# A transformer block with a routed feed-forward layer: three pieces of TensorE's order put elsewhere

## What is computed

```python
q = x @ wq_lat @ wq_heads            # k and v alike; 16 heads of 8
att = softmax(where(causal, q @ k.T * SCALE, -inf))
x = x + layernorm((att @ v) @ w_proj + b_proj)
ys = geglu(xn @ Ws1 + bs1) @ Ws2 + bs2           # shared part; geglu(a, g) = a * gelu(g)
top_val, top_idx = top_k((xn @ Wr + br) / 1.5, 2)
yr = sum over the two experts of softmax(top_val) * (geglu(xn @ We1[e] + be1[e]) @ We2[e] + be2[e])
x = x + layernorm(ys + yr)
```

## Time and profile before

| | us |
|---|---|
| median of 3 runs | 1270.77 |
| lowest and highest | 1266.59, 1272.27 |
| the profiled execution | 1269.61 |
| its span, first to last instruction | 1267.8 |

### The profile page before, as it was taken

The page is one execution under the profiler, slowest core; times in us unless marked ns, Lnnn a source line. Parts: engine busy times, 40 slices in busy tenths (PEclk is TensorE's granted clock), DMA queues, the critical chain, the costliest instruction groups (busy, mean ns, idle before and its releaser), DMA issues.

```text
span 1267.8 us, 31490 instructions
## 1 busy us (share of the span) xinstructions
PE 1074.8 (85%) x8446; PEld 619.5 (49%) x8446; DVE 837.0 (66%) x2411; ACT 745.3 (59%) x1311; POOL 631.4 (50%) x1184
## 2 busy tenths in 40 slices
PE   4789999999999999978888877655899999999765
PEld 2633333333333333323565545322788888888732
DVE  7587777777878777766875556322466666666637
ACT  3777777777767777756544344321566666666616
POOL 4256666666666666644145545554144444444344
PEclk9799999999999999989767887778899999999988
DMA  8223333333333333332611111111222222221156
GB/s 221 69 74 88 96 101 101 91 90 97 95 94 93 96 101 99 91 104 62 223 31 39 37 37 35 37 37 56 51 67 61 62 66 60 62 67 51 47 192 215
DMA packets 135607, 107.47 MB, mean 85 GB/s; under 512 B 32204, under 2 KB 127875, under 8 KB 135539
## 3 DMA queue, kind: packets, MB, share of 16 engines
q1 hardware_dynamic: 124722, 87.45, 24.6%
q0 software_dynamic: 8544, 17.78, 3.9%
q10 hardware_dynamic: 2272, 1.45, 0.4%
HBM read 55.96 MB, written 50.69 MB: 84 GB/s over the span
## 4 chain that ended last, share of the span: by engine, by line
PE 62%; DVE 10%; issue 9%; another core or an unknown queue 7%; ACT 7%; DMA 3%; SPq 1%; ACTq 1%; POOL 0%; DVEq 0%; POOLq 0%
PE ps L1221 11%; PE ps L1386 7%; PE ps L1387 7%; PE ps L1398 7%; DVE maxima L1524 5%; PE ps L1149 5%; PE ps L1180 5%; PE ps L1140 2%; PE ps L1313 2%; PE ps L1332 2%; PE ps L1157 2%; ACT quad_area L973 2%; PE ps L1203 1%; ACT outT_area L918 1%
## 5 line engine op out<-in xcount | busy, mean ns | idle before, releaser
L1524 DVE TENSOR_REDUCE maxima<-ps 128x8 f32<-128x1024 f32 x320 | 387.0, 1222 | 122.6 <-PE ps L1149 109.3
L911 ACT ACTIVATE pT_area<-ps 128x1024 f32<-128x1024 f32 x320 | 327.5, 1025 | 145.1 <-PE ps L1180 144.5
L699 POOL TENSOR_SCALAR_AFFINE_SELECT pT_area<-pT_area 128x256 f32<-128x256 f32 (+1 forms) x448 | 190.4, 439 | 110.9 <-ACT pT_area L911 109.1
L801 POOL DMA_INDIRECT ys_dram<-quad_area,place_cur x139 | 133.1, 957 | 206.3 <-issue 138.2
L791 POOL DMA_INDIRECT xs_dram<-quad_area,idx_cur x128 | 123.3, 963 | 139.5 <-issue 73.0
L1221 PE MATMUL ps<-pT_area,quad_area 128*32 128x512 f32 (+3 forms) x2048 | 190.9, 446 | 0.0
L1180 PE MATMUL ps<-quad_area 64*128 64x512 bf16 (+3 forms) x1024 | 124.9, 301 | 25.5 <-DVE maxima L1524 22.2
L1386 PE MATMUL ps<-quad_area 128*128 128x256 f32 (+1 forms) x456 | 129.8, 367 | 8.1 <-issue 6.8
L1387 PE MATMUL ps<-quad_area 128*128 128x256 f32 (+1 forms) x456 | 128.4, 363 | 0.0
L1149 PE MATMUL ps<-quad_area 61*128 61x128 bf16 (+2 forms) x1792 | 126.8, 244 | 0.0
L1819 DVE SCALAR_TENSOR_TENSOR quad_area<-ps,be_cur,xnT 128x256 f32<-128x256 f32 (+1 forms) x228 | 97.5, 458 | 40.2 <-ACT xnT L1009 37.1
(11 more groups left out here) (237 smaller groups left out, 1665.0 us busy)
## 6 DMA issues: line engine op xcount, KB each, us to landing
qk_dram<-split_area SPq DMA_DIRECT2D x192, 128.0 KB, 2.3
quad_area<-qk_dram SPq DMA_DIRECT2D x256, 96.0 KB, 2.3
row_area<-xs_dram SPq DMA_DIRECT2D x63, 132.0 KB
pT_area<-ys_dram SPq DMA_DIRECT2D x16, 512.0 KB, 5.2
pT_area<-in_L_ffn_We SPq DMA_DIRECT2D x12, 384.0 KB, 7.5
out_dram<-pT_area SPq DMA_DIRECT2D x7, 512.0 KB, 2.9
xs_dram<-row_area SPq DMA_DIRECT2D x5, 528.0 KB, 4.2
split_area<-in_L_ffn_We SPq DMA_DIRECT2D x12, 192.0 KB, 3.8
```

The source lines that it names most:

```text
L699: return pool.affine_select(out=blocks, in_=blocks, compare_op=ALU.is_ge, fill=0.0, base=0, pattern=[[0, count], [1, P]], channel_multipli ...
L801: pool.indirect_dma_start(ys_dram, at, ys[:, ns % 2, h, :], None).then_inc(s_yst[ns % 2], 16)
L911: act.activation(pT[:, gs % 2, n, :], ps[:, bank:bank + 2, :].rearrange("p a b -> p (a b)"), ACT.Exp).then_inc(s_exp, 1)
L1524: dve.tensor_reduce(to, ps[:, bank:bank + 2, :].rearrange("p a (j k) -> p a j k", k=P), AX, ALU.max).then_inc(s_mxf, 1)
```

## The change

Three pieces of PE's order move.

1. The third value product (kb 2) of a quad stood behind exp 4, a step after the quad's own; now it stands behind max 0 of the step after that, so behind `project` too where there is one.
2. The turn of the maxima stood behind exp 1; from step 0 on it now stands behind max 2, the next item.
3. The shared layer's second product is done a step later (batch n-9 in step n), and stands ahead of the turn of rows. ACT's copy of it (L958) follows. The stage gets one more step, which holds the last product alone; the padding copies stay in the step where they were.

```diff
-PRODUCTS = {("exp", 0): (2, 3), ("exp", 2): (1, 0), ("exp", 3): (1, 1), ("exp", 4): (1, 2)}
+PRODUCTS = {("max", 0): (2, 2), ("exp", 0): (2, 3), ("exp", 2): (1, 0), ("exp", 3): (1, 1)}
...
-        STEPS = B + 8
+        STEPS = B + 9
...
-                if ns == STEPS - 1:
+                if ns == B + 7:
                     pad(act, range(1, E, 2))
...
-                if 0 <= ns - 8 < B:
-                    act.wait_ge(s_y2, n - 7)
-                    act.activation(tiles4(ysum, n - 8), ps[:, Y2, :].rearrange("p (t c) -> p t c", c=C), ACT.Copy).then_inc(s_ysum, 1)
+                if 0 <= ns - 9 < B:
+                    act.wait_ge(s_y2, n - 8)
+                    act.activation(tiles4(ysum, n - 9), ps[:, Y2, :].rearrange("p (t c) -> p t c", c=C), ACT.Copy).then_inc(s_ysum, 1)
...
-                    if (kind, n) == ("exp", 1) and present("max_rows", gs):
+                    if (kind, n) == (("exp", 1) if gs < 0 else ("max", 2)) and present("max_rows", gs):
                         turn_maxima(gs, g)
...
                 if 0 <= ns < B:
                     turn_y(ns, n)
+                if 0 <= ns - 9 < B:
+
+                    par = (ns - 9) % 2
+                    pe.wait_ge(s_hid, 2 * n - 16)
+                    ge(pe, s_ysum, n - 9)
+                    bias(Y2, 1)
...
                 if 0 <= ns - 3 < B:
                     if ns == 3:
                         pe.wait_ge(s_yq, QUADS)
...
-                if 0 <= ns - 8 < B:
-
-                    par = ns % 2
-                    pe.wait_ge(s_hid, 2 * n - 14)
-                    ge(pe, s_ysum, n - 8)
-                    bias(Y2, 1)
```

More of the change, by code:

```diff
@@ L1295, in shared @@
                     turn_y(ns, n)
+                if 0 <= ns - 9 < B:
[3 more added lines that the diff above has]
+                    bias(Y2, 1)
+                    for t in range(NT):
+                        for j in range(2):
+                            last = pe.matmul(ps[:, Y2, t * C:(t + 1) * C], hid[:, par, j, t * P:(t + 1) * P], ws2[:, j, :],
+                                             start=False, stop=(t == NT - 1 and j == 1))
+                    last.then_inc(s_y2, 1)
                 if 0 <= ns - 3 < B:
@@ L1304, in shared @@
                     last.then_inc(s_xT2, 1)
-                if 0 <= ns - 8 < B:
-                    par = ns % 2
-                    pe.wait_ge(s_hid, 2 * n - 14)
-                    ge(pe, s_ysum, n - 8)
-                    bias(Y2, 1)
-                    for t in range(NT):
-                        for j in range(2):
-                            last = pe.matmul(ps[:, Y2, t * C:(t + 1) * C], hid[:, par, j, t * P:(t + 1) * P], ws2[:, j, :],
-                                             start=False, stop=(t == NT - 1 and j == 1))
-                    last.then_inc(s_y2, 1)
                 if 0 <= ns - 3 < B:
```

## The result

The changed kernel takes 1292.53 us (median of 4 executions, 1291.65 to 1303.58) where the kernel before, run beside it, takes 1268.68. The difference of the medians is 24 us. The ratio is 1.0211, with a 95% interval of 1.0156 to 1.0266, so the loss lies between some 20 and 34 us. The forecast was 1278.0 with a range of 1258 to 1288: the right sign, less than half of the size, and the measured time is above the range.

A forecast was written before the change was run, and what follows sets the result against it. It took PE and, after the projection, DVE's maxima to bound attention, and a 14.91 us loop through POOL's scatters the shared stage. Sum: 1269.61 + 8.4 (value product) + 0 + 0 = 1278.0 us, range 1258 to 1288.

The forecast's parts named there:

- Third value product: Attention: moving it behind max 0 costs +0.60 us per four-step loop (0.35 to 0.70), 14 times, +8.4 us.
- Turn of the maxima: Attention: the wait ahead of max 2 goes, but exp 2 still waits for DVE's second maximum; 0 us.
- Second product: Shared stage: scatters hold the second gelu's signal, so steps stay 14.91 us; 0 us, ends -5 and +8.
- first rival: "Merged scatters", shared stage: short steps alternate with long holds, +1.2 for each of four pairs, +3 at end; 1286, chance 0.17.
- The second rival: Shared stage: PE's backlog, not scatters, is the hold, so moving the second product shortens steps; 1250, chance 0.17.
- One more step: End of shared stage: the last second product and its copy, 0.60 us on ACT, hidden by 2.8 us; 0.

The follow-up runs named there:

- g4: Kernel before with the third value product behind max 0 only in steps that follow no projection: 1258.52 us (one execution).
- e1: Kernel before with only the third value product moved behind max 0: 1283.64 us, ratio 1.0069.
- e2: Kernel before with only the turn of the maxima moved behind max 2: 1255.15 us, ratio 0.9866.
- e3: Kernel before with only the shared layer's second product moved a step later, with the added step: 1272.89 us, ratio 1.0058.
- p1: Kernel before without the shared layer's second product except its bias row (shared output missing from the result): 1258.81 us (one execution).
- p2: Kernel before with four idle masks on POOL between the fourth and fifth scatter of each batch: 1241.67 us (one execution).
- g1: Kernel before with the turn of the maxima behind max 2 and four idle POOL masks between fourth and fifth scatter: 1237.50 us, ratio 0.9799.
- g3: As g1, with three idle masks in place of four: 1230.70 us, ratio 0.9750.
- e4: Changed kernel with the third value product back behind exp 4, the other parts kept: 1269.42 us, ratio 0.9986.
- f2: As e2, with POOL waiting ahead of each batch's scatters until PE's a product of this step is done: 1256.03 us, ratio 0.9911.
- h3: Changed kernel, all three parts, with three idle POOL masks in the middle of each batch's scatters: 1254.84 us, ratio 0.9910.
- h1: As g3, with two idle masks in place of three: 1243.65 us, ratio 0.9831.
- h2: As g3, with the three idle masks ahead of a batch's first scatter in place of ahead of the fifth: 1232.57 us (one execution).

## Why the prediction fell short

**Third value product: right in place and mechanism, 3 us too small.** It said +0.60 per loop. The wait ahead of max 0 was forecast at 0.99 and is 0.96; the waits on L1157 for DVE were forecast at 12.6 and are 12.4; exp 2 comes 3.98 us behind max 0, 0.67 later than before. The joins of like steps are 34.47 apart where 34.3 was forecast. The term that was mis-sized is the loss per loop: 0.80, of which 0.67 is the step after the second projection, 0.10 is the step after it, without a projection, which I had put at nothing (g4), and 0.04 lies in the step with `gs` mod 4 of 1. Fourteen times 0.80 is 11.2, and the first L973 is 11.5 later. That these agree so closely is in part luck: e1, with the same loop, has 14.9. The upper bound of 0.70 was too low since only one step had been worked through.

**Turn of the maxima: right in attention.** 0 us, with ACT's wait turned into DVE's; e1 and the changed kernel have the same loop, e2 and before too. That alone it would make the whole kernel 13 us faster, by way of the shared stage's last bursts, no term of the sum had.

**Second product: the step that failed.** The working said that the second gelu's signal is held until the scatters end, so that the second product, which isn't in the loop, changes nothing: 0 us with +8 as its end. The hold was right and its rule was wrong. A signal is not held for the whole burst: those of PE's first matmuls in it come within 2 us (the second g product of the changed kernel is over by 689.43, its gelu starts at 691.29), and those of later ones wait. In the eight equal steps of the kernel before the second gelu's g product was on the late side, and that is why 14.91 stood eight times. The change let the second product run ahead, the first gelu came 4.9 us earlier, the second one's signal slipped through at 7.2 us into the burst, and the next eight scatters joined on. This was the first rival ("merged scatters"), whose condition and shape came true: short steps that alternate with long holds. It had been given 0.17, on the ground that the eight equal steps showed no signal getting through; but those steps were of the order before, and the prediction itself had noted that the first gelu would come 2 to 3.5 us earlier. Its price was near in all and wrong in its parts: it had four pairs at +1.2 and +3 at the end, 7.8. The trace has two pairs, 10.6 + 24.9 = 35.5 and 35.9, against 29.8, partly given back by the steps around them, +3.7 by the last L973, and +6.3 behind it. The shared stage lost 10.0 and not 0. That the place of the second product makes the alternation is shown by e3; that all of the 6.3 are its doing is not, since the last bursts move by 9 to 13 us with other small changes too.

**The second rival** (PE's backlog of its own work) is out: less work of PE did not shorten the steps by as much (p1), and more work of POOL did shorten them (p2, g1, g3). And e3 and e4, with the product out of the way, got longer stages and not shorter ones. The Trainium skill's rule that a matmul's end is an estimate and its signal goes out once PSUM has acknowledged the writes (page "Perfetto Trace Analysis", section "Tensor Engine Instruction (MATMUL, LD_WEIGHTS)") may hold; it doesn't explain the 2.5 us of the earlier trace rows, which come and go with POOL's scatters.

**One more step:** forecast 0, measured 1.0 in this trace; e3 and e4, which have the step too, start the first expert tile 19.1 and 18.8 us behind the last scatter, so it is between 0 and 1.0. The first expert tile is now 19.87 us behind the last scatter instead of 18.88, and waits for the last copy of the second product:

```profile
913.14 0.60 ACT L958 ACTIVATE y_sb<-ps 128x512 f32<-128x512 f32 x1 [4.47 <-PE ps L1304]
```

```profile
913.79 0.69 PE L1374 MATMUL ps<-ident,row_area 128*128 128x128 f32 x2 [0.69 <-ACT y_sb L958]
```

**Sum.** 1269.61 + 11.5 + 10.0 + 1.0 - 0.3 (experts and final stage) = 1291.8, which is the changed kernel's profiled execution. The parts are read from one trace of each kernel and have to give its sum; they are no check of it.

**Open:** which way the last bursts fall in a given execution. The kernel before ranges over 25 us, and e2, f2 and g4, whose attention is all but the same, had a shared stage 9 to 13 us shorter; so part of the 10.0 may be of this kind. With a pause in the scatters the executions of one kernel lie within 4 and 7 us (g1, g3), but within 17 in h3, and no run takes that end of the stage by itself. The new order's second product and the moved value product may act on it as the turn does. Open too is what POOL's scatters do inside the chip that PE's signals wait for.

## What to carry to other kernels

Where a step's time is the same eight times over, ask what keeps it there before moving work around it: it may be a hold that your change unlocks, and a shorter step can start the next one's transfers on top of the last one's. When an engine's finished work is seen late by others, look at what a third engine issues at that moment; a pause there can be worth more than any order on the waiting engines. And a product that fills an engine's wait is worth about its own length in that place (here 0.67 us for a product of 0.57): work through every step that it leaves, not only the one where the wait is largest.

## What the runs showed of the hardware

While POOL issues scatters (0.96 us each, 1.27 apart), signals of PE's matmuls that end late in the burst reach ACT only after it: 2.48 us after the last of sixteen in the changed kernel (707.01 against 704.53), 1.63 into a pause in p2, 2.26 behind the last of eight in h1. Signals of matmuls early in a burst pass, one as late as 7.2 us into it (691.29). That how many pass depends on how much PE finishes in the burst fits p1 and h2, and is not shown by itself. DVE got one signal of PE 12 us late and still ahead of the end (702.80), and one of its own 1.17 us late (697.05). Where in the chip they are held no trace shows.

A pause of 1.7 us in the middle of eight scatters lets the second product's signal out (g3), one of 1.1 us does not: the scatters go on 0.9 us before it comes (h1: 702.94 against 703.82). With the pause of 1.7 us the kernel (g3) takes 1230.7 us, 37 below the kernel before and 62 below the changed one, though POOL does more.
